# Attention over 1601 keys: adding the maximum's shift for two tiles of keys at once, in four row quarters of TensorE

## The reference, cut to what matters

```
Q = (layernorm(x) @ W_Q + b_Q)          # 32 x 64 x 256, as 16 heads of 16
K = (ctx @ W_K + b_K); V = (ctx @ W_V + b_V)   # 32 x 1601 x 256
scores = einsum('bhld,bhsd->bhls', Q, K) / sqrt(16)
attn = softmax(scores, axis=-1)
out = x + einsum('bhls,bhsd->bhld', attn, V) @ W_O + b_O
```

## Time and profile before

| | us |
|---|---|
| median of three runs | 2286.67 |
| span of the profiled execution | 2286.7 |
| TensorE busy in that span | 2115.3 (93%) |
| VectorE busy | 1428.2 (62%) |
| ScalarE busy | 1240.8 (54%) |
| GpSimd busy | 764.9 (33%) |

### The profile page before, as it was taken

The page is one execution under the profiler, slowest core; times in us unless marked ns, Lnnn a source line. Parts: engine busy times, 40 slices in busy tenths (PEclk is TensorE's granted clock), DMA queues, the critical chain, the costliest instruction groups (busy, mean ns, idle before and its releaser), DMA issues. The chain is left out here.

```text
span 2286.7 us, 65088 instructions
## 1 busy us (share of the span) xinstructions
PE 2115.3 (93%) x28676; PEld 1741.5 (76%) x28676; DVE 1428.2 (62%) x2619; ACT 1240.8 (54%) x1680; POOL 764.9 (33%) x571
## 2 busy tenths in 40 slices
PE   7999999999999999999999999788699997699993
PEld 5888889999999999999989988544132337599993
DVE  6545555555555555555555553436788875688885
ACT  3445555555555555555555555168799981365551
POOL 2232232232232232232222220000799972265551
PEclk9899999999999999999999999899799998799997
DMA  3111111111111111111111110214874531666663
GB/s 107 45 43 40 41 49 40 41 50 40 41 50 40 41 49 40 41 49 40 41 44 42 37 41 7 66 55 152 227 177 137 147 85 43 224 217 212 217 231 124
DMA packets 131138, 195.41 MB, mean 85 GB/s; under 512 B 18116, under 2 KB 109252, under 8 KB 130696
## 3 DMA queue, kind: packets, MB, share of 16 engines
q1 hardware_dynamic: 121832, 174.98, 25.6%
q0 software_dynamic: 4416, 12.06, 1.6%
q10 hardware_dynamic: 4608, 4.20, 0.5%
HBM read 159.61 MB, written 31.59 MB: 84 GB/s over the span
## 5 line engine op out<-in xcount | busy, mean ns | idle before, releaser
L560 DVE TENSOR_REDUCE max_part<-work 128x1 f32<-128x384 f32 (+1 forms) x1024 | 535.3, 569 | 175.8 <-PE work L688 152.0
L623 ACT ACTIVATE probs<-scores 128x1024 f32<-128x1024 f32 (+1 forms) x416 | 423.7, 1026 | 333.0 <-PE scores L713 321.6
L235 POOL TENSOR_TENSOR ctx_lo<-ctx_whole,ctx_hi 128x768 fp32r<-128x768 f32 (+1 forms) x128 | 231.8, 1811 | 997.5 <-DVE ctx_hi L229 962.4
L555 DVE SCALAR_TENSOR_TENSOR keys_lo<-work,bk,keys_hi 128x384 fp32r<-128x384 f32 (+1 forms) x256 | 162.7, 635 | 329.1 <-ACT keys_hi L602 329.1
L1332 POOL TENSOR_TENSOR decay<-steps_in,xn 128x1024 f32<-128x1024 f32 x126 | 243.7, 1970 | 135.7 <-POOLq L940 116.1
L707 PE MATMUL scores<-q_hi,keys_hi 64*128 64x256 f32 (+1 forms) x1664 | 252.5, 283 | 2.2 <-issue 1.5
L707 PE MATMUL scores<-q_hi,keys_lo 64*128 64x256 f32 (+1 forms) x1664 | 249.2, 278 | 0.8 <-issue 0.8
L707 PE MATMUL scores<-q_lo,keys_hi 64*128 64x256 f32 (+1 forms) x1664 | 249.3, 278 | 0.6 <-issue 0.5
L678 PE MATMUL work<-wv_hi,ctx_hi 128*128 128x256 f32 (+1 forms) x832 | 244.8, 294 | 0.1
L678 PE MATMUL work<-wv_hi,ctx_lo 128*128 128x256 f32 (+1 forms) x832 | 234.9, 282 | 0.0
L678 PE MATMUL work<-wv_lo,ctx_hi 128*128 128x256 f32 (+1 forms) x832 | 234.8, 282 | 0.0
(11 more groups left out here) (233 smaller groups left out, 4608.0 us busy)
## 6 DMA issues: line engine op xcount, KB each, us to landing
xs<-in_w_T SPq DMA_DIRECT2D x46, 1024.0 KB, 7.7
ctx_whole<-in_ctx_T SPq DMA_DIRECT2D x96, 384.0 KB, 3.2
steps_in<-scratch_results SPq DMA_DIRECT2D x256, 128.0 KB, 2.7
ctx_whole<-in_ctx_T SPq DMA_DIRECT2D x32, 449.0 KB, 3.4
scratch_results<-steps SPq DMA_DIRECT2D x16, 512.0 KB, 2.6
scratch_mixed<-mixed ACTq DMA_DIRECT2D x32, 128.0 KB, 3.3
scratch_z<-z SPq DMA_DIRECT2D x16, 256.0 KB, 3.7
zg<-scratch_z SPq DMA_DIRECT2D x16, 256.0 KB, 3.2
```

Source lines behind the costliest of these rows:

```text
L235: nc.gpsimd.tensor_tensor(s.ctx_lo[c][:, :, 0:n], s.ctx_whole[c % 2][:, :, 0:n], s.ctx_hi[c][:, :, 0:n].bitcast(F32), ALU.subtract).then_i ...
L555: nc.vector.scalar_tensor_tensor(keys_lo[par][:, m, start:start + n], bank[:, 0:n], s.bk[:, m:m + 1], keys_hi[par][:, m, start:start + n]. ...
L560: nc.vector.reduce_max(max_part[par][:, place(pair), c:c + 1], bank[:, 0:CHUNKS[c][1]], AX) \
L623: nc.scalar.activation(probs[n % PROBS][0:rows, :], scores[slot][0:rows, :], ACT.Exp, scale=1.0 / HD ** 0.5).then_inc(exp_done, 1)
```

## The change

TensorE no longer adds the shift inside score. It computes the scores of both tiles of a pair, with the maxima units between them as before, and then a new function shift adds the shift for both tiles: four matmuls of 512 columns, each on one quarter of 32 rows, two quarters for the first tile of the pair and two for the second, into four different banks. The last of the four tells ScalarE that both tiles are ready. Tile 12, which is alone, uses quarters 0 and 1. The wait for the shifts of a batch stands ahead of these four. So that the negative maxima lie in all four quarters, VectorE's reduction is made twice, for the upper and the lower half of neg_max, and own_pair gets its ones in rows 0 to 3 of every quarter.

```diff
+SHIFT_ROWS = 32
+def shift_rows(slot, h):
+    first = (2 * slot + h) * SHIFT_ROWS
+    return slice(first, first + SHIFT_ROWS)
@@ VectorE, after the last maxima unit
-                        nc.vector.tensor_reduce(
-                            neg_max[:, :].rearrange("p (h x) -> p h x", h=2)[:, :, 0:4],
-                            max_part[par][:, :, :].rearrange("p (h x) c -> p h x c", h=2), AX, ALU.max, negate=True) \
-                            .then_inc(maxima_done, 1)
+                        for slot in range(2):
+                            nc.vector.tensor_reduce(
+                                neg_max[:, :].rearrange("p (s h x) -> p s h x", s=2, h=2)[:, slot, :, 0:4],
+                                max_part[par][:, :, :].rearrange("p (h x) c -> p h x c", h=2), AX, ALU.max,
+                                negate=True).then_inc(maxima_done, 1)
@@ VectorE, once at the start
-            nc.vector.tensor_tensor(own_pair[:, :], s.ident[:, 0:4], s.ident[:, SIDE:SIDE + 4], ALU.add)
+            nc.vector.tensor_reduce(own_pair[:, :], s.ident[:, :].rearrange("p (r x) -> p x r", x=SHIFT_ROWS)[:, 0:4, :],
+                                    AX, ALU.add).then_inc(shift_made, 1)
-            dve.wait_ge(shift_made, 1)
+            dve.wait_ge(shift_made, 2)
@@ TensorE, the row unit
-                    pe.wait_ge(maxima_done, b + 1)
+                    pe.wait_ge(maxima_done, 2 * b + 2)
@@ TensorE, score and shift
-                if t == 0:
+            def shift(b, par, tiles):
+                if tiles[0] == 0:
                     wait_evacuated(pe, b, ROW)
-                for h in range(2):
-                    last = nc.tensor.matmul(bank[0:rows, h * BANK:(h + 1) * BANK], ones[side(h), 0:rows],
-                                            shifts[side(h), :], start=False, stop=True, skip_group_check=True)
-                last.then_inc(scores_ready, 1)
+                for slot, t in enumerate(tiles):
+                    rows, bank = TILES[t][1], scores[(par * NT + t) % 2]
+                    for h in range(2):
+                        last = nc.tensor.matmul(bank[0:rows, h * BANK:(h + 1) * BANK], ones[shift_rows(slot, h), 0:rows],
+                                                shifts[shift_rows(slot, h), :], start=False, stop=True,
+                                                skip_group_check=True)
+                last.then_inc(scores_ready, len(tiles))
@@ TensorE, attend
                         score(b, par, t)
+                    shift(b, par, tiles)
                     if ahead:
```

More of the change, by code:

```diff
@@ L706, in score @@
                             at = column(g * HPG)
-                            last = nc.tensor.matmul(bank[0:rows, at:at + GCOLS], k[par][side(g), m, start:start + rows],
-                                                    q[par][side(g), m, :], start=(m == 0 and n == 0), stop=False,
-                                                    skip_group_check=True)
-                if t == 0:
-                    wait_evacuated(pe, b, ROW)
-                for h in range(2):
-                    last = nc.tensor.matmul(bank[0:rows, h * BANK:(h + 1) * BANK], ones[side(h), 0:rows],
-                                            shifts[side(h), :], start=False, stop=True, skip_group_check=True)
-                last.then_inc(scores_ready, 1)
+                            nc.tensor.matmul(bank[0:rows, at:at + GCOLS], k[par][side(g), m, start:start + rows],
+                                             q[par][side(g), m, :], start=(m == 0 and n == 0), stop=False,
+                                             skip_group_check=True)
+            def shift(b, par, tiles):
+                if tiles[0] == 0:
+                    wait_evacuated(pe, b, ROW)
+                for slot, t in enumerate(tiles):
[3 more added lines that the diff above has]
+                                                shifts[shift_rows(slot, h), :], start=False, stop=True,
+                                                skip_group_check=True)
+                last.then_inc(scores_ready, len(tiles))
             def mix(b, par, t):
```

## The result

The changed kernel takes 2348.3 us, the median of four runs (2342.61 to 2353.76), against 2286.95 us of the kernel before: a ratio of 1.0263, 95% interval 1.0248 to 1.0278 (the two medians alone give 1.0268). The direction was forecast, the size was not: 2318 us was given, with a range from 2264 to 2338.

What follows compares the result with a forecast made beforehand. TensorE, busy 1313.78 of 1324 us, was taken as the bound. 0.20 + 0.12 + 0.31 + 0.19 = 0.82 us a batch, 31 times: 25 us; with 6 for the last batch, 2286.7 became 2318 us, range 2264 to 2338.

Steps and rivals of the forecast that it cites:

- The twelve changes of the row tile: Switches between 64 and 32 rows around the shifts, added in every batch: 2.28 us at 0.19 each.
- the 1.38 us saved: One of two shift steps removed in six pairs, 6 x 0.23 us a batch.
- The bound of 0.19 us: Cost taken for a change between 64 and 32 rows, from bounds of 0 and 0.19.
- (a): Rival: no cost between 64 and 32 rows, VectorE becomes the limit, 2267 us; chance 0.15.
- (b): Rival: changes cost half, weights loaded ahead but array emptied, -0.32 us a batch, 2282 us; chance 0.10.
- rival (c): The four quarters run only two at a time, 43 us on top, 2361 us; chance 0.09.
- the sum for a place, 2.71 us: Pairs 1 to 4, first maxima to the unit behind: 2.66 us before, 2.71 after, +0.05 each.
- pair 5: VectorE works without a break, so the second score's late half ends as before; +0.31 us a batch.
- pair 0: Later exponentials on ScalarE delay the keys' copies, low part and next maxima: +0.12 us a batch.
- the last batch: Without units between pairs, scores wait for later exponentials: +1.9 us in each of three groups, about 6 us.
- what costs nothing: Second reduction covered by values matmuls, new multiplicand made once, later wait for shifts, ScalarE late only as TensorE.
- would make the prediction wrong: Quarters' weight loads beginning during the last scores, or a ScalarE wait counted as covered ending last in pairs 1 to 4.

Runs made afterwards that it cites:

- Changes alone: Kernel before, its order kept, each tile's shift right behind its scores but in quarters of 32 rows: 2421.9 us (one run).
- the last experiment: Kernel before, the values unit behind pair 5 and the two maxima ahead of tile 12 swapped: 2268.9 us, ratio 0.9931.

## Why the prediction was right or wrong

**Right: the mechanism, and its price.** The twelve changes of the row tile outweigh the 1.38 us saved. The bound of 0.19 us for a change between 64 and 32 rows, taken from rows between 64 and 128, holds: 0.20 against a step of 0.12, and a record of 0.50 against 0.39, in the changed kernel, and a period of 47.05 us where 47.0 was worked out for changes alone. Rivals (a) and (b) fall with it. (That the maxima would follow 0.3 us behind the quarters' start was a slip: the sum's own terms, 0.10, 0.23 and 0.09, make 0.42, and 0.44 was measured.) The direction was not luck either: with the wait described below taken away, the kernel still takes 2315 us. The rule of the Trainium skill, "TensorEngine Tiling (Array Packing)", Key Properties, that a change of tiling mode drains TensorE, agrees with the rows between 64 and 32 rows too, where the change costs 0.19 us.

**Right: the four quarters run together.** 0.44 us from the start of four to the maxima behind them, where two take 0.43 ("Changes alone"); rival (c) falls. The estimate of 0.30 instead of 0.23 us for four, worked out from a figure of the Trainium skill, "TensorE: Matmul & The Clock Gate", Part 3, was too high: in this trace four lose nothing against two.

**Wrong: pairs 1 to 4.** The step that failed is the sum for a place, 2.71 us, and in it the second "scores 0.70". The place measured 2.97, and the second score 1.00 with the change of row tile behind it, where 0.79 was counted (0.70 and the 0.09 up to the shift's start). I had put the third and fourth maxima straight behind the first score, 0.23 us earlier than before, and looked only at VectorE's readiness for the unit behind the pair, not at the bank of the fourth maxima itself. For pair 5 the prediction does ask when VectorE frees the bank of those maxima; for pairs 1 to 4 it does not. Before, the first tile's shift lay in between and covered that wait; by moving it the change took the cover away. A weight load that started 0.10 us late under the shift now starts 0.21 us late with nothing to hide it, and the shift of both tiles waits for the half that is late. Issued 0.23 us later, the same maxima give 2.78 us and a kernel of 2315 us, close to the 2318 of the prediction: the sum was that of a kernel without this wait. What is left between 2.71 and 2.78 are terms taken 0.01 to 0.02 us too small (a score has 0.71, the shift up to the maxima 0.44).

Mean lengths of the places of a batch, between 510 and 1050 us, changed kernel less kernel before, and what was forecast:

| place | forecast, us | measured, us |
|---|---|---|
| pair 0, first scores to next maxima | +0.12 | +0.06 |
| pairs 1 to 4, first maxima to unit behind, together | +0.20 | +1.20 |
| pair 5, first maxima to values | +0.31 | +0.35 |
| tile 12, first maxima to values | +0.19 | +0.14 |
| a batch | +0.82 | +1.75 |

Pairs 1 to 4 alone are 1.00 us a batch more than forecast. The whole is 0.93 more, and 31 times that is 29 of the 30 us by which the prediction was short of the median.

**Pair 5, right.** Here the prediction held that VectorE's pace would keep the second score's late half where it was, and it did: the shift's records start 737.82 - 735.39 = 2.43 us behind the pair's first maxima, and in the kernel before the late half's shift 717.16 - 714.82 = 2.34 behind them, to which the change adds 0.09. But that end is not fixed by VectorE alone. With the maxima issued later the place got 0.24 us shorter: fewer steps of the second score then stand behind the held unit.

**Pair 0, right in kind.** The exponentials are late and the keys' copies queue behind them, as the rows of ScalarE, VectorE and TensorE in pair 0 of the changed kernel show:

```profile
703.57 1.94 ACT L634 ACTIVATE probs<-scores 128x1024 f32<-128x1024 f32 x2 [1.67 <-PE scores L728]
705.40 1.06 ACT L613 ACTIVATE keys_hi<-work,bk 128x384 fp32r<-128x384 f32 x2
```
```profile
706.02 1.14 DVE L564 SCALAR_TENSOR_TENSOR keys_lo<-work,bk,keys_hi 128x384 fp32r<-128x384 f32 x2 [5.80 <-ACT keys_hi L613]
```
```profile
707.31 0.44 PE L699 MATMUL work<-keys_hi,q_hi 64*128 64x384 f32 x2
```

The two copies run back to back (1.06 for both, where the earlier trace rows had an idle of 0.47 between them), the low parts end at 707.16 and the maxima start 0.15 later, as in the earlier trace rows. Back to back they start 0.46 us apart, not the 0.58 I had used, so the place lost less than the 0.12 forecast.

**Right: the last batch.** 6 us forecast, 6.3 measured. Each group of four tiles was to take 1.9 us longer; the first exponentials of two groups are 1477.64 - 1469.42 = 8.22 us apart, and were 1424.88 - 1418.56 = 6.32 before. 3.4 of the 6.3 us are back when each tile's shift follows its own score. **Right: what costs nothing.** In pairs 1 to 4 ScalarE did not become the limit: with the skew gone the period fell to the sum of TensorE's steps. The second reduction stayed covered, as one batch of the changed kernel shows (both reductions in one row, then the row unit):

```profile
697.42 0.28 DVE L574 TENSOR_REDUCE neg_max<-max_part 128x8 f32<-128x32 f32 x2
```
```profile
698.72 0.38 PE L704 MATMUL work<-ident,neg_max 128*128 128x128 f32 x2
```

They end at 697.70, 1.0 us before the row unit.

The chances put 0.75 on slower, rightly; the range ended at 2338 because its upper end was made of changes of 0.25 us alone. A wait that the move itself uncovers was among what "would make the prediction wrong" only for ScalarE.

## What to carry to other kernels

Taking a step out of a TensorE stream moves everything behind it earlier, and each of those instructions must be checked for its own buffers: here a step of 0.23 us moved away brought a unit to a bank that VectorE had not yet freed. Look at what a step covers before you move it. Count changes of the row tile as work, 0.19 us each in this kernel, not much less than a shift step; packing four small matmuls into quarters saved 0.23 us a pair here and cost up to 0.38, so what counts is the row tile of the work around them. Order work so that matmuls of one row tile stand together, as the last experiment did for 16 us. And where a list of waits names an engine that was done long before, look for another cause of the idle time.

## What the runs showed of the hardware

The two row halves of TensorE run on apart once one of them is held: behind the late maxima one half stayed 0.21, then 0.18 us behind the other through six steps of scores. The half ahead lost 0.04 us in its first step (723.02 to 723.17) and nothing after, and the loss came due only at the first instructions that needed both (the quarters, or a unit of 128 rows). In the rows that make this plain, single matmuls stand where pairs stood. What waits for a bank is the weight load, not the matmul alone: the bank was free 0.05 us after the other half's maxima had begun (722.89 and 722.84), and the held half came 0.21 us late.
